# Layer 0's time and channel mix: normalised row copies moved from VectorE to ScalarE

## The reference, cut to what matters

```
x = x + _L0_attn_ref(_layernorm(x), ...)

h  = layernorm(x, ln1_g, ln1_b)          # of the normalised x
hs = time_shift(h)                       # one step back, zeros first
k, v, r = mixes of h and hs by tm_k, tm_v, tm_r, times Wk, Wv, Wr
y  = wkv(time_decay, time_first, k, v)   # recurrence over the 32 steps
x1 = x + (sigmoid(r) * y) @ Wo.T
h2 = layernorm(x1, ln2_g, ln2_b)
k2, r2 = mixes of h2 and its shift by cm_k, cm_r
out = x1 + sigmoid(r2 @ Wcr.T) * (relu(k2 @ Wck.T) ** 2 @ Wcv.T)
```

## Time and profile before

| | us |
|---|---|
| time, median of 3 runs | 1788.74 (1781.33 to 1790.08) |
| span of the profiled execution | 1784.8 |
| the stage `l0_mixes` within it | about 182 to 466 |
| VectorE busy over the whole span | 1284.3 (72%) |
| ScalarE busy over the whole span | 1023.9 (57%) |
| TensorE busy over the whole span | 1366.9 (77%) |

### The profile page before, as it was taken

One profiled execution on the slowest core, in us unless ns is written; L12 is line 12 of the kernel. 1 busy time (PEld: TensorE's weight loads), 2 busy tenths in 40 slices (PEclk: granted clock), 3 DMA queues, 4 the chain that ended last, 5 costly groups with the idle time before them and its releaser, 6 DMA issues. The chain is left out here.

```text
span 1784.8 us, 33601 instructions
## 1 busy us (share of the span) xinstructions
PE 1366.9 (77%) x12612; PEld 774.9 (43%) x12612; DVE 1284.3 (72%) x2312; ACT 1023.9 (57%) x1851; POOL 765.9 (43%) x808
## 2 busy tenths in 40 slices
PE   6999347988679887787865947435788799699898
PEld 4544123655544355555542322001344445355566
DVE  3598899971368765777668639999999899985200
ACT  1676324433443476878662446533797798885553
POOL 2355000000232434434414006666798788877443
PEclk9999667989779978878967977556899899999999
DMA  6397200000145567668612348998664575550000
GB/s 253 145 355 274 89 0 0 1 1 0 67 138 167 180 115 132 124 117 143 87 40 90 97 119 214 242 226 203 144 164 110 120 168 126 127 135 20 1 13 12
DMA packets 152516, 212.37 MB, mean 119 GB/s; under 512 B 107199, under 2 KB 112255, under 8 KB 139296
## 3 DMA queue, kind: packets, MB, share of 16 engines
q1 hardware_dynamic: 152356, 210.23, 46.3%
HBM read 155.37 MB, written 31.75 MB: 105 GB/s over the span
## 5 line engine op out<-in xcount | busy, mean ns | idle before, releaser
L2807 POOL TENSOR_TENSOR mf_st<-mf_st,mf_c_rep 128x1024 f32<-128x1024 f32 x128 | 301.1, 2353 | 199.4 <-DVE mf_st L2875 199.2
L2875 DVE TENSOR_TENSOR_SCAN mf_st<-mf_dA,mf_u_ps 128x512 f32<-128x512 f32 x256 | 310.1, 1212 | 0.0
L2698 PE MATMUL mf_y_ps<-mf_st,c_consts 128*32 128x512 f32 x512 | 128.7, 719 | 131.0 <-POOL mf_st L2807 95.2
L2986 ACT ACTIVATE mf_dA<-c_dt,c_neg_a 128x496 f32<-128x496 f32 x256 | 163.8, 699 | 67.7 <-DVE mf_st L2875 67.1
L2869 DVE TENSOR_TENSOR mf_u_ps<-mf_st,mf_b_ps 128x512 f32<-128x512 f32 x256 | 177.7, 694 | 20.1 <-DMA mf_st<-xs 8.7
L2830 POOL TENSOR_TENSOR mf_hid<-mf_g,mf_hid 128x512 f16<-128x512 f32 x128 | 148.9, 1165 | 96.8 <-ACT mf_g L3003 96.5
L3000 ACT ACTIVATE mf_hid<-mf_eh,c_vecs 128x512 f16<-128x512 f32 x128 | 88.0, 687 | 123.6 <-PE mf_eh L2749 123.2
L2749 PE MATMUL mf_eh<-mf_parts,mf_w 128*128 128x512 f16 x480 | 122.8, 394 | 22.4 <-POOL mf_parts L2826 20.5
L259 POOL TENSOR_TENSOR c_parts<-mg_ln_hT,c_parts 128x512 f16<-128x512 f32 x8 | 9.1, 1155 | 303.7 <-ACT c_parts L250 303.7
L2111 DVE TENSOR_REDUCE t_mx<-t_s_ps 128x2 f32<-128x514 f32 x128 | 87.9, 687 | 54.1 <-PE t_s_ps L1997 53.8
L2769 PE MATMUL mf_ey<-mf_w,mf_hid 128*128 128x256 f16 x960 | 120.3, 276 | 0.0
(11 more groups left out here) (514 smaller groups left out, 3015.5 us busy)
## 6 DMA issues: line engine op xcount, KB each, us to landing
mf_st<-xs SPq DMA_DIRECT2D x64, 1024.0 KB, 7.2
a_ctx_t<-in_ctx_t SPq DMA_DIRECT2D x16, 1024.0 KB, 8.9
a_ctx_n<-in_ctx_n SPq DMA_DIRECT2D x16, 1024.0 KB, 8.0
cqs<-a_whole_rows SPq DMA_DIRECT2D x16, 512.0 KB, 6.6
mo_raw<-in_l_w SPq DMA_DIRECT2D x16, 512.0 KB, 4.1
ws<-mo_split SPq DMA_DIRECT2D x32, 256.0 KB, 2.6
c_cq<-cqs SPq DMA_DIRECT2D x16, 512.0 KB, 4.7
mf_w<-ws SPq DMA_DIRECT2D x20, 256.0 KB, 11.6
```

The source lines that it names most:

```text
L2698: m = e.matmul(y_ps[T * j:T * j + T, :], c.pick[:, gg, :], st[u % RING][:, j, :], start=(gg == 0), stop=(gg == 3))
L2807: e.tensor_tensor(half(u, h), half(u, h), over(c_rep[u // UNITS % 2][:, :], [P, 2, BT], 1), ALU.mult).then_inc(hcs("done"), 1)
L2875: e.tensor_tensor_scan(st[u % RING][:, j, :], dA[:, n % AHEAD, :], u_ps[j % 2][:, :], 0.0, ALU.mult, ALU.add).then_inc(hs("done"), 1)
L2986: e.activation(by_batch(dA[:, n % AHEAD, :])[:, :, 1:], dt, ACT.Exp, scale=c.neg_a[:, at:at + 1]).then_inc(dAs("done"), 1)
```

## The change

The scaled copies of the rows are no longer made by VectorE (48 instructions fewer there) but by ScalarE, as one ACTIVATE with the function Identity, the row's rstd as scale and -mean * rstd as bias. VectorE only works out the reciprocals and these offsets, one small instruction for each norm, and does so between the scans and the outputs of the recurrence, for which `wkv_states` is cut in two (`wkv_outputs` is its second half). On ScalarE the copies stand behind the two roots and ahead of `squared`. TensorE's order is as it was; its transposes wait for ScalarE's counters `f_norm` and `g_norm` instead of VectorE's. In the diff, `front_scale` and the first two loops' pieces are VectorE's, the new `front_norm` and the last piece ScalarE's.

```
-            def front_norm(i):
-                plain = xn0[i % 2]
+            def front_scale(i):
                 e.wait_ge(*f_root.at("std", i))
                 e.reciprocal(f_rstd[:, :, :].rearrange("p a k -> p (a k)"),
                              f_std[:, :, :].rearrange("p a k -> p (a k)")).then_inc(front("rstd"), 1)
                 e.wait_ge(*front.at("rstd", i))
                 e.tensor_tensor(f_rstd[:, 1, :], f_rstd[:, 0, :], f_rstd[:, 1, :], ALU.mult).then_inc(front("rstd2"), 1)
-                e.wait_ge(*f_turn.at("done", i - 1))
                 e.wait_ge(*front.at("rstd2", i))
-                for to, a, name in ((xn, 1, "norm"), (plain, 0, "plain")):
-                    for k in range(KT_):
-                        e.tensor_scalar(to[:, k, :], c.X[:, i * KT_ + k, :], f_mean[:, k:k + 1], f_rstd[:, a, k:k + 1],
-                                        ALU.subtract, ALU.mult).then_inc(front(name), 1)
+                e.scalar_tensor_tensor(f_off[:, :, :], f_rstd[:, :, :], -1.0, over(f_mean[:, :], [P, 2, KT_], 1), ALU.mult,
+                                       ALU.mult).then_inc(front("offset"), 1)
...
+            def wkv_outputs(i):
+                V = wkv
                 e.wait_ge(*V.at("bb", i))
                 e.wait_ge(*exps.at("z4", i))
...
                 if some(i):
                     wkv_states(i)
                 if some(i + 1):
-                    front_norm(i + 1)
+                    front_scale(i + 1)
                 if some(i - 1):
-                    chan_norm(i - 1)
+                    chan_scale(i - 1)
                 if some(i):
+                    wkv_outputs(i)
                     wkv_ratio(i)
...
+            def front_norm(i):
+                e.wait_ge(*front.at("offset", i))
+                e.wait_ge(*f_turn.at("done", i - 1))
+                for to, a, name in ((xn, 1, "norm"), (xn0[i % 2], 0, "plain")):
+                    for k in range(KT_):
+                        e.activation(to[:, k, :], c.X[:, i * KT_ + k, :], ACT.Identity, bias=f_off[:, a, k:k + 1],
+                                     scale=f_rstd[:, a, k:k + 1]).then_inc(f_norm(name), 1)
...
                 if some(i - 1):
                     chan_root(i - 1)
+                if some(i + 1):
+                    front_norm(i + 1)
+                if some(i - 1):
+                    chan_norm(i - 1)
                 if some(i - 2):
                     squared(i - 2)
                     chan_gate(i - 2)
```

More of the change, by code:

```diff
@@ L758, in l0_mixes @@
         f_var, f_mean, f_inv = sb("f_var", [P, 2, KT_]), sb("f_mean", [P, KT_]), sb("f_inv", [P, KT_])
-        f_std, f_rstd = sb("f_std", [P, 2, KT_]), sb("f_rstd", [P, 2, KT_])
+        f_std, f_rstd, f_off = (sb(f"f_{k}", [P, 2, KT_]) for k in ("std", "rstd", "off"))
         xn0 = [sb(f"xn0{u}", [P, KT_, C]) for u in range(2)]
@@ L772, in l0_mixes @@
         g_var, g_mean = sb("g_var", [P, KT_]), sb("g_mean", [P, KT_])
-        g_std, g_rstd = sb("g_std", [P, KT_]), sb("g_rstd", [P, KT_])
+        g_std, g_rstd, g_off = (sb(f"g_{k}", [P, KT_]) for k in ("std", "rstd", "off"))
         gn, gT, gd = sb("gn", [P, KT_, C]), sb("gT", [P, CJ, BT]), sb("gd", [P, N])
@@ L785, in l0_mixes @@
         STATS = [("stats", KT_), "sums", "diff", "between", "variance", "mean"]
-        front = steps("front", STATS + ["veps", "vinv", "var2", "rstd", "rstd2", ("norm", KT_), ("plain", KT_), "shift", "first",
+        front = steps("front", STATS + ["veps", "vinv", "var2", "rstd", "rstd2", "offset", "shift", "first",
                                         ("mix", 3 * CJ)])
@@ L790, in l0_mixes @@
         xi = steps("xi", [("added", CJ)])
-        chan = steps("chan", STATS + ["rstd", ("norm", KT_), "shift", "first", ("mix", 2 * CJ)])
+        chan = steps("chan", STATS + ["rstd", "offset", "shift", "first", ("mix", 2 * CJ)])
         close = steps("close", [("rkv", 2), ("plus", 2), ("added", 2)])
@@ L795, in l0_mixes @@
         exps = steps("exps", ["z2", "z1", "z3", "z4"])
+        f_norm, g_norm = steps("f_norm", [("norm", KT_), ("plain", KT_)]), steps("g_norm", [("norm", KT_)])
         g_root, g_feat = steps("g_root", ["std"]), steps("g_feat", [("features", CJ)])
@@ L882, in _ @@
                 if some(i + 1):
-                    turn("turn", i + 1, xn, front, f_turn)
+                    turn("turn", i + 1, xn, f_norm, f_turn)
                 if i == -1:
@@ L1049, in chan_norm @@
                 e.wait_ge(*chan.at("rstd", i))
[L1050 to L1053, removed]
+                e.scalar_tensor_tensor(g_off[:, :], g_rstd[:, :], -1.0, g_mean[:, :], ALU.mult,
+                                       ALU.mult).then_inc(chan("offset"), 1)
             def chan_mix(i):
@@ L1121, in chan_root, with chan_norm @@
                 e.activation(g_std[:, :], g_var[:, :], ACT.Sqrt, bias=c.eps[:, 0:1]).then_inc(g_root("std"), 1)
+            def front_norm(i):
[5 more added lines that the diff above has]
+                                     scale=f_rstd[:, a, k:k + 1]).then_inc(f_norm(name), 1)
+            def chan_norm(i):
+                e.wait_ge(*chan.at("offset", i))
+                e.wait_ge(*g_turn.at("done", i - 1))
+                for k in range(KT_):
+                    e.activation(gn[:, k, :], XI[i % 2][:, k, :], ACT.Identity, bias=g_off[:, k:k + 1],
+                                 scale=g_rstd[:, k:k + 1]).then_inc(g_norm("norm"), 1)
             def exponentials(i):
@@ L1168, in chan_gate @@
                                  ACT.Sigmoid).then_inc(gates("done"), 1)
-            for each in (f_root, f_feat, lin_out, exps, g_root, g_feat, relus, squares, gates):
+            for each in (f_root, f_norm, f_feat, lin_out, exps, g_root, g_norm, g_feat, relus, squares, gates):
                 each.start(e)
```

4 lines of the change are left out of this document (2 added, 2 removed).

## The result

| | before | after |
|---|---|---|
| time, median of 5 runs on one chip (us) | 1787.02 (1781.33 to 1790.08) | 1799.91 (1794.08 to 1805.73) |
| ratio after / before, 95% interval | | 1.0071 (1.0046 to 1.0096) |
| span of the profiled execution | 1784.8 | 1797.9 |
| the stage, from its first instruction on a tc_ tile to the next stage's first | 285.0 | 294.0 |
| all the rest of the span | 1499.8 | 1503.9 |

The change makes the kernel slower by 0.7%. The stage is 9.0 us longer, the rest of the program 4.1. The profiled execution after took 1799.91 us, 2.0 more than its span.

A forecast was written before the change was run, and what follows sets the result against it. VectorE paces pass 1, VectorE and TensorE are full in pass 2, and delay at cv(1) reaches the end. 8.0 us waits + 1.5 clock = +9.5, span 1784.8 to 1794.3, plus 3.9 to the median: 1798, range 1789 to 1806.

The forecast's parts named there:

- The signs named in the prediction: Trace marks: ScalarE, TensorE and VectorE waits, y(3) at about 396; fails if cv(0) starts before 319 or cv(1) before 368.
- Pass -1: Block 0's features stand behind eight copies on ScalarE, done at 193.9; VectorE went on at 192.50 before: cost 1.4 us.
- VectorE into pass 2: VectorE saves 2.5 us in pass 0 and 3.7 in pass 1, less 1.4: it enters pass 2 4.8 us early.
- Price of a copy: One scaled copy on ScalarE takes 592 ns, overlapping by 0.10 in a row: 0.50 us each, bounds 0.32 to 0.59.
- Offsets and copies in pass 2: Front offsets at 307.4, twelve copies on ScalarE until 313.4, so relus begin 7.4 us later and squares end at 321.6.
- cv(0), forecast +3.8: TensorE in pass 2: cv(0) waits for the last square and starts at 321.6 instead of 317.84, 3.8 us later.
- VectorE's two waits in pass 2: VectorE waits 4.4 us for block 3's features and about 4.1 for cv(0) at the second gate product; all gain gone.
- Pass 3: Channel offsets at 362.2, squares done at 372.5; cv(1), gated(3), y(3) and the end come 8.0 us late.
- The clock: TensorE's idle time of about 4 us before cv(1) lowers its granted clock: 1.5 us, bounds 0 and 2.7.
- The rival of one delay only: Pass 3's squares are not late by themselves, cv(1) starts at 368, end +4, near 1793; chance 0.15.
- The rival of a longer slow clock: TensorE stays at half clock into cv(0) and cv(1), two losses of 2.7: +13, 1802 and up; chance 0.09.
- The faster rival: Squares don't hold TensorE in pass 2, first relu before 310; VectorE keeps 9.6 us, 1779; chance 0.06.

The follow-up runs named there:

- e1: Changed kernel with ScalarE's relus and squares of block i-2 moved ahead of the copies; 1782.66 us, ratio to before 0.9975, stage 277.0.
- e2: Changed kernel with the copies made by VectorE again from pass 2 on; 1782.32 us, ratio to before 0.9975, stage 277.9.
- e3: Changed kernel with VectorE's offsets worked out behind the three recurrence outputs instead of ahead; 1804.94 us, ratio to before 1.0091, stage 298.8.
- e6: Changed kernel with copies by ScalarE in passes -1 to 2, by VectorE from pass 3 on; one run, 1791.17 us, stage 287.0.
- e7: Changed kernel with copies by VectorE in pass 2 alone, by ScalarE in all others; one run, 1787.03 us, stage 287.0.
- e5: Changed kernel with ScalarE's copies made by Copy without scale and offset, so rows are not normalised; one run, 1798.99 us, stage 287.8.
- e4: Changed kernel again without edit, on the chip of e1, e2 and e3; 1801.18 us, ratio to before 1.0077, stage 293.4.
- e8: e1 with VectorE's gated product also moved ahead of the closing and channel mix; 1773.69 us, ratio to before 0.9919, stage 267.6.
- e9: Kernel before, with only VectorE's gated product moved ahead of the closing and channel mix; 1780.62 us, ratio to before 0.9958, stage 276.9.
- n1: Kernel before with the change's new tiles and semaphores allocated but not used; 1786.6 us, ratio to before 0.9998, stage 285.1.
- n0: Kernel before, unchanged, timed against itself; 1783.81 us, ratio 0.9993, stage 285.2.

## Why the prediction was right, step by step

The forecast was 1798, slower in about half of the cases; it came to 1799.91, slower. The mechanism is shown by e1, e2, e3, e6 and e7: squares that stand behind copies which wait for VectorE's offsets, TensorE waiting for the squares, and a price in the clock on top. The signs named in the prediction came true: cv(0) at 319.75 and cv(1) at 370.82, where it would have failed before 319 and 368.

That the number came so close is in part luck. In the stage the waits were forecast at 8.0 and the clock at 1.5, 9.5 in all. Up to y(3) 6.3 and 1.7 were measured, so y(3) stands at 394.96 and not at about 396, and 1.0 more came behind it from the clock, where the forecast had nothing: 9.0. The rest of the program, which the forecast took as unchanged, is 4.1 longer in the profile, so the span is 3.6 above the forecast (1797.9 for 1794.3). And the 3.9 us from the span to the median were too much: the median of all five runs before stands 2.2 above that span, and after it is 2.0. That took back 1.9 of the 3.6.

- **Pass -1, forecast +1.4.** Block 0's shift starts 1.1 later (188.98 + 4.63 = 193.61 against 192.50). VectorE enters pass 0 only 0.7 later (198.70 + 4.63 = 203.33 against 202.67), since the linear of block 0 took 6.15 us instead of 6.61.
- **VectorE into pass 2, forecast 4.8 early.** It was 6.4 early (282.24 + 4.63 = 286.87 against 293.24). The copies' removal was priced right for pass 1, which shrank by 3.8 against 3.7 worked out. Mis-sized was what pass -1 cost (0.7 for 1.4) and what pass 0 gave (3.2 for 2.5). e5 shows too that the entry into pass 0 hangs on the linear of block 0: there the copies are shorter by 1.5, the shift is earlier by 1.2 and the entry by 2.1, with that linear at 5.22 instead of 6.15.
- **Price of a copy, forecast 0.592 alone and 0.50 in a row.** Measured 0.588 and (4.04 - 0.588) / 7 = 0.493. Plain ones take 0.402, so two operands cost 0.186. The Trainium skill, ScalarE: Activation LUTs, section What ACT_TABLE_LOAD costs, has 93 ns for each per-row operand and for the overlap; the trace agrees, with 186 for two operands and 95 for the overlap.
- **Offsets and copies in pass 2, forecast 307.4 and six us.** The offset stood at 305.49 (300.86 + 4.63) and the twelve copies took 5.91. The relus started 5.6 late instead of 7.4 and the squares ended 1.9 earlier than forecast. 1.6 of that is VectorE's earlier entry.
- **cv(0), forecast +3.8.** Measured +1.9. The forecast saw 3.0 us of cover ahead of cv(0), so that cr(0) could be slow for nothing. (Between the end of cr(0) and cv(0) its own numbers leave 4.0, and 3.0 behind the transposes.) cr(0) took 6.28 at a granted clock of 0.57 (3.62 at 1.00 before), and only 0.28 was left. It cost nothing, as said, but barely.
- **VectorE's two waits in pass 2, forecast 4.4 and 4.1.** Measured 4.00 and 4.47; the second stands on the second gate product only, as forecast. All the gain but 1.4 us went here (entry to pass 3 at 337.44 + 4.63 = 342.07 against 343.50).
- **Pass 3, forecast cv(1) +8.0.** Measured +6.3, 1.7 less, again VectorE's lead: offsets at 360.47 where 362.2 was said.
- **The clock, forecast +1.5.** For cv(1), of which the term spoke, this was nearly right: 15.77 for 14.08, +1.7. Left out were the two later places that run at the low clock already before the change: y(3) took 0.5 less (5.93 for 6.41), and ck(3) 1.5 more (16.99 for 15.53, behind the same wait of 5.04). With them the stage is 6.3 + 1.7 - 0.5 + 1.5 = 9.0 longer, of 9.5 forecast.
- **The rival of one delay only** was to give +4; each delay alone leaves the stage 2.0 above before (e6, e7). The rival of a longer slow clock was to give +13, with the full 2.7 in cv(0) and in cv(1); cv(0) took 14.08 at a clock of 1.00, and cv(1) lost 1.7. **The faster rival** hung on ScalarE reaching its first relu before 310 in pass 2; it reached it at 311.6. Freed from the copies, as in e1, it is worth 8.0. The prediction also held that the move pays only where ScalarE has nothing queued behind. In e1 gates and features stand behind the copies, and it pays: what counts is whether TensorE waits for what stands behind them.

What stays open: the program lost more than the stage. The span grew by 13.1, of which 9.0 is the stage; the medians differ by 12.9. In e4 it is 13.8 (0.77% of 1787.93) against 8.4 in the stage, and in e1, e2, e3, e8 and e9 too the ratio gives 0.6 to 3.5 us more than the stage (e1: 0.25% or 4.5 us are gained, 8.0 in the stage). Each of these differences is inside its interval, but they all have one sign. The single run of e5 is the farthest off, 11.0 us above the median of before on its chip with a stage 2.8 longer. n1, at 0.9998 (0.9981 to 1.0016), gives no sign that the allocations do it. In the profiles the program's last stage took 733.9 to 734.4 us with before's instructions and 734.8 to 742.2 in all others, and attention's stage in layer 1 went the other way (325.8 after, 330.9 before), but it varies by as much with before's own instructions (329.4 in n0, 320.2 in n1). The span without the stage is 1487.5 to 1500.0 us in the three profiles with before's instructions, 1503.9 and 1496.9 in the two of the changed kernel, and 1497.9 to 1509.2 in the others. Runs of one and the same kernel lie up to 18 us apart, so single profiles can't settle this, and it wasn't tried further.

## What to carry to other kernels

Before work goes to the emptier engine, read what stands behind its new place in that engine's queue and who waits for that. A copy that waits for another engine makes everything behind it wait as well, and a busy share of 57%, or the 36% that ScalarE has in the stage itself (103.7 of 284.6 us), says nothing of it: here the same copies made the stage 9 us longer ahead of the squares and 8 us shorter behind them. Where one engine of a pipeline waits for a single instruction of another, like TensorE's y(3) for gated(3), look for what stands in front of that instruction without need. That paid another 8 to 9 us here.
